# Causal attention: diagonal key blocks put together into steps of 512 columns, 34 steps per set instead of 40

## What is computed

```python
# layer 0
scores = sips_alpha[0] * jnp.tanh(raw / sips_beta[0])      # raw = q k^T
scores = scores + lam * hamming[:, None, :, :]             # feature products
scores = scores + lat
scores = jnp.where(causal[None, None], scores, -jnp.inf)
attn = jax.nn.softmax(scores, axis=-1)
# layer 1
scores = jnp.einsum('bqhd,bkhd->bhqk', q, k) * scale
scores = jnp.where(causal, -jnp.inf, scores)
attn = jax.nn.softmax(scores, axis=-1)
```

## Time and profile before

| | |
|---|---|
| median of 3 runs | 4454.76 us (4454.74 to 4455.85) |
| the profiled execution | 4471.63 us, its span 4469.8 us |
| mean granted PE clock | 0.959 of full speed |
| PE busy | 3854.6 us, 86% of the span |
| ACT busy | 3432.6 us, 77% |
| DVE busy | 2840.0 us, 64% |
| layer 0 attention | from 316 us (first tanh) to 2494 us |
| layer 1 attention | from 3032 us (first exp) to 4152 us |

### The profile page before, as it was taken

One profiled execution on the slowest core, in us unless ns is written; L12 is line 12 of the kernel. 1 busy time (PEld: TensorE's weight loads), 2 busy tenths in 40 slices (PEclk: granted clock), 3 DMA queues, 4 the chain that ended last, 5 costly groups with the idle time before them and its releaser, 6 DMA issues. The chain is left out here.

```text
span 4469.8 us, 66988 instructions
## 1 busy us (share of the span) xinstructions
PE 3854.6 (86%) x21966; PEld 1406.6 (31%) x21966; DVE 2840.0 (64%) x5324; ACT 3432.6 (77%) x3144; POOL 450.8 (10%) x407
## 2 busy tenths in 40 slices
PE   6958888888888888888888776758999999999787
PEld 2422222222222222222222463432222222222465
DVE  5637777777777777777777796872233332332588
ACT  2429999999999999999999412337999999999333
POOL 3520000000000000000000124650000000000133
PEclk9979999999999999999999888988999999999899
DMA  5851111112111112111111345562222222222332
GB/s 174 260 175 53 48 52 39 42 48 57 43 52 42 42 49 56 44 50 41 39 56 30 115 141 155 169 187 77 72 73 60 79 66 71 75 58 65 98 92 85
DMA packets 307816, 360.48 MB, mean 81 GB/s; under 512 B 56590, under 2 KB 237934, under 8 KB 307249
## 3 DMA queue, kind: packets, MB, share of 16 engines
q1 hardware_dynamic: 307508, 356.62, 27.4%
HBM read 228.15 MB, written 128.25 MB: 80 GB/s over the span
## 5 line engine op out<-in xcount | busy, mean ns | idle before, releaser
L835 DVE SCALAR_TENSOR_TENSOR att_prob<-att_tanh,alpha,ps 128x512 f32<-128x512 f32 (+3 forms) x2560 | 1569.5, 661 | 525.4 <-ACT att_tanh L775 333.9
L716 PE MATMUL ps<-att_q,att_k 99*128 99x512 bf16 (+7 forms) x5120 | 1196.7, 355 | 173.6 <-DMA att_v<-v_ones 79.1
L743 PE MATMUL ps<-att_prob,att_v 128*32 128x512 f32 (+3 forms) x10240 | 1215.1, 547 | 10.2 <-ACT att_prob L785 5.3
L775 ACT ACTIVATE att_tanh<-ps,rbeta 128x2048 f32<-128x2048 f32 (+3 forms) x640 | 1102.9, 1723 | 123.3 <-PE ps L716 123.3
L781 ACT ACTIVATE att_prob<-ps 128x1024 f32<-128x1024 f32 (+3 forms) x1280 | 1051.9, 920 | 78.4 <-PE ps L716 70.1
L785 ACT ACTIVATE att_prob<-att_prob 128x2048 f32<-128x2048 f32 (+3 forms) x640 | 1065.6, 1665 | 52.1 <-DVE att_prob L835 49.6
L725 PE MATMUL ps<-att_f,att_g 75*128 75x512 bf16 (+3 forms) x2560 | 854.0, 361 | 177.9 <-DVE att_prob L835 153.3
L716 PEld LDWEIGHTS ps<-att_q,att_k 96*128 96x128 bf16 (+1 forms) x5120 | 396.8, 99 | 1045.4 <-ACT att_prob L781 430.4
L823 DVE TENSOR_TENSOR att_prob<-att_prob,keep 128x256 f32<-128x256 f32 x512 | 211.5, 423 | 647.3 <-ACT att_prob L781 642.2
L725 PEld LDWEIGHTS ps<-att_f,att_g 75*128 75x128 bf16 x2560 | 235.7, 97 | 1060.8 <-DVE att_prob L835 1029.1
L743 PEld LDWEIGHTS ps<-att_prob,att_v 128*32 128x32 f32 x10240 | 202.5, 108 | 391.8 <-issue 147.2
(11 more groups left out here) (132 smaller groups left out, 2470.9 us busy)
## 6 DMA issues: line engine op xcount, KB each, us to landing
att_k<-k_parts SPq DMA_DIRECT2D x768, 64.0 KB
att_q<-q_parts SPq DMA_DIRECT2D x768, 64.0 KB
v_ones<-proj_vs SPq DMA_DIRECT2D x128, 256.0 KB, 3.1
att_v<-v_ones SPq DMA_DIRECT2D x128, 256.0 KB
post_o<-o_t SPq DMA_DIRECT2D x40, 512.0 KB, 5.1
att_f<-f_parts SPq DMA_DIRECT2D x384, 48.0 KB
o_t<-att_on SPq DMA_DIRECT2D x512, 32.0 KB, 1.9
q_parts<-proj_parts SPq DMA_DIRECT2D x32, 384.0 KB, 4.1
```

The costliest lines, as they stand in the source:

```text
L716: mm = pe.matmul(ps[:, bank, off:TG], keys, q_s[:, n % QU, h, off:TG], start=True, stop=True)
L743: mm = pe.matmul(ps[VW * h:VW * (h + 1), O0 + n % 2, off:TG], v_s[:, c % KU, kb % CB, h * VW:(h + 1) * VW], prob[:, S % R, h, off:TG], sta ...
L775: th.done(act.activation(tanh_s[:, S % 2, :, off:TG], ps[:, QK0:QK0 + HQ, off:TG], ACT.Tanh, scale=kn["rbeta"][:, 0:1]))
L835: sc.done(dve.scalar_tensor_tensor(prob[:, S % R, h, off:TG], tanh_s[:, S % 2, h, off:TG], kn["alpha"][:, 0:1], ps[:, E0 + h % 2, off:TG], ...
```

## The change

The order of the steps within a set comes from a new function, `even_steps`, and a step is now a list of pieces (group, key block, first query, first column, width) and a list of the columns at which a mask block lies. The 384-wide and the 128-wide diagonal block of a group form one step of 512 columns; the 256-wide blocks of groups g-1 and g (g odd) form one, placed behind the first key block of group g. So a set has 24 steps off the diagonal, 4 of the first diagonal block, 4 of 384 + 128 and 2 of 256 + 256: 34 steps, all of 512 columns. Counted from 0, groups 0 to 3 begin at steps 0, 2, 9 and 19 of the set (before: 0, 4, 12 and 24). Group 0 has its last step at step 3, group 1 at 8, group 2 at 20 and group 3 at 33.

ACT and DVE instructions of layer 0 take the whole width. PE has the same matmuls as before, per piece: in a step of two pieces there are 8 for scores, 8 for extra and 8 of masks, and 16 recorded ones for weigh. In layer 1 the two mask blocks of a pair of heads are one DVE instruction (128 x 512 elements). `normalise` does one part per step throughout in layer 0. All lookaheads, numbers of banks and buffers, and SP's order are as they were.

```diff
@@ -30,6 +30,7 @@
 GB = T // TG
 TT = TG // P
 KB = T // P
+CB = TG // P
 HQ = 4
 NHQ = H // HQ
 NF = 12
@@ -604,21 +605,39 @@
     return n
+def even_steps():
+    steps = []
+    for g in range(GB):
+        d = g * CB
+        for kb in range(d):
+            steps.append(([(g, kb, 0, 0, TG)], []))
+            if kb == 0 and g % 2 == 1:
+                steps.append(([(g - 1, d - 2, 2 * P, 0, 2 * P), (g, d + 2, 2 * P, 2 * P, 2 * P)], [0, 2 * P]))
+        steps.append(([(g, d, 0, 0, TG)], [0]))
+        steps.append(([(g, d + 3, 3 * P, 0, P), (g, d + 1, P, P, 3 * P)], [0, P]))
+    return steps
 def attend_phase(nc, kn, layer):
-    steps = [(g, kb) for g in range(GB) for kb in range((g + 1) * (TG // P))]
+    steps = even_steps()
     NST = len(steps)
+    ends = [[g for g in range(GB) if max(i for i, (ps_, _) in enumerate(steps) if any(p[0] == g for p in ps_)) == s] for s in range(NST)]
+    kept_at = [sum(1 for _, m in steps[:s] if m) for s in range(NST)]
     N_SET = B * NHQ
     N = N_SET * NST
     NG = N_SET * GB
-    ND = GB * (TG // P)
+    ND = sum(1 for _, m in steps if m)
     R = 4
     LAG = 2
     QU, KU = 3, 6
-    CB = TG // P
     QK0, E0, O0 = 0, 4, 6
     SR, FR = (QROWS, FROWS + 3) if layer == 0 else (QROWS + 3, 0)
     with ExitStack() as ctx:
@@ -654,10 +673,12 @@
         def at(S):
             it, s = divmod(S, NST)
-            g, kb = steps[s]
-            r = kb - g * CB
-            off = r * P if r > 0 else 0
-            return it, g, kb, off, r >= 0, kb == (g + 1) * CB - 1
+            return (it, s) + steps[s]
+        def blocks(t, masked):
+            first, step = masked[0], masked[1] - masked[0] if len(masked) > 1 else P
+            return t[..., first:first + step * len(masked)].rearrange("... (m n) -> ... m n", n=step)[..., 0:P]
         @block.sync
         def _(sp):
@@ -702,9 +723,9 @@
             pe.wait_ge(ones_in, 16)
             def scores(S, pair):
-                it, g, kb, off, diag, _ = at(S)
-                n, c = it * GB + g, it * GB + kb // CB
-                if kb == 0 and pair == 0:
+                it, _, pieces, _ = at(S)
+                if pieces[0][1] == 0 and pair == 0:
+                    n = it * GB + pieces[0][0]
                     pe.wait_ge(stacks_in[n % QU], (n // QU + 1) * (16 * N_LOAD))
                 if layer == 1:
                     pr.wait(pe, 2 * S + pair - 3)
@@ -712,35 +733,39 @@
                     th.wait(pe, S - 1)
                 for h in (2 * pair, 2 * pair + 1):
                     bank = QK0 + (h if layer == 0 else 2 * ((2 * S + pair) % 3) + h % 2)
-                    keys = k_s[:, c % KU, h, (kb % CB) * P:(kb % CB + 1) * P]
-                    mm = pe.matmul(ps[:, bank, off:TG], keys, q_s[:, n % QU, h, off:TG], start=True, stop=True)
+                    for g, kb, q0, col, w in pieces:
+                        n, c = it * GB + g, it * GB + kb // CB
+                        keys = k_s[:, c % KU, h, (kb % CB) * P:(kb % CB + 1) * P]
+                        mm = pe.matmul(ps[:, bank, col:col + w], keys, q_s[:, n % QU, h, q0:q0 + w], start=True, stop=True)
                 if layer == 1 or pair == 1:
                     qk.done(mm)
             def extra(S, h):
-                it, g, kb, off, diag, _ = at(S)
-                n, c = it * GB + g, it * GB + kb // CB
+                it, _, pieces, masked = at(S)
                 sc.wait(pe, S * HQ + h - 2)
-                mm = pe.matmul(ps[:, E0 + h % 2, off:TG], g_s[:, c % KU, (kb % CB) * P:(kb % CB + 1) * P], f_s[:, n % QU, h, off:TG], start=True, stop=not diag)
-                if diag:
-                    mm = pe.matmul(ps[:, E0 + h % 2, off:off + P], kn["identb"][:], kn["mask_kq"][:], start=False, stop=True)
+                for g, kb, q0, col, w in pieces:
+                    n, c = it * GB + g, it * GB + kb // CB
+                    mm = pe.matmul(ps[:, E0 + h % 2, col:col + w], g_s[:, c % KU, (kb % CB) * P:(kb % CB + 1) * P], f_s[:, n % QU, h, q0:q0 + w], start=True, stop=not masked)
+                    if masked:
+                        mm = pe.matmul(ps[:, E0 + h % 2, col:col + P], kn["identb"][:], kn["mask_kq"][:], start=False, stop=True)
                 ex.done(mm)
             def weigh(S):
-                it, g, kb, off, diag, last = at(S)
-                n, c = it * GB + g, it * GB + kb // CB
+                it, s, pieces, masked = at(S)
                 if layer == 0:
                     pr.wait(pe, S)
-                elif diag:
-                    kept.wait(pe, (it * ND + kb) * 2 + 1)
+                elif masked:
+                    kept.wait(pe, (it * ND + kept_at[s]) * 2 + 1)
                 else:
                     pr.wait(pe, S * 2 + 1)
-                if kb == 0:
-
-                    o_tr.wait(pe, n - 2)
-                for h in range(HQ):
-                    mm = pe.matmul(ps[VW * h:VW * (h + 1), O0 + n % 2, off:TG], v_s[:, c % KU, kb % CB, h * VW:(h + 1) * VW], prob[:, S % R, h, off:TG], start=kb == 0, stop=last)
+                for g, kb, q0, col, w in pieces:
+                    n, c = it * GB + g, it * GB + kb // CB
+                    if kb == 0:
+                        o_tr.wait(pe, n - 2)
+                    for h in range(HQ):
+                        mm = pe.matmul(ps[VW * h:VW * (h + 1), O0 + n % 2, q0:q0 + w], v_s[:, c % KU, kb % CB, h * VW:(h + 1) * VW], prob[:, S % R, h, col:col + w], start=kb == 0, stop=g in ends[s] and (g, kb) == [p[:2] for p in pieces if p[0] == g][-1])
                 pv.done(mm)
             scores(0, 0)
@@ -768,21 +793,19 @@
             for S in range(N + 1):
                 if S < N:
-                    it, g, kb, off, *_ = at(S)
                     if layer == 0:
                         qk.wait(act, S)
                         sc.wait(act, (S - 2) * HQ + HQ - 1)
-                        th.done(act.activation(tanh_s[:, S % 2, :, off:TG], ps[:, QK0:QK0 + HQ, off:TG], ACT.Tanh, scale=kn["rbeta"][:, 0:1]))
+                        th.done(act.activation(tanh_s[:, S % 2], ps[:, QK0:QK0 + HQ], ACT.Tanh, scale=kn["rbeta"][:, 0:1]))
                     else:
                         for pair in range(2):
                             qk.wait(act, S * 2 + pair)
                             bank = QK0 + 2 * ((2 * S + pair) % 3)
                             pv.wait(act, S - R)
-                            pr.done(act.activation(prob[:, S % R, 2 * pair:2 * pair + 2, off:TG], ps[:, bank:bank + 2, off:TG], ACT.Exp, scale=float(HD) ** -0.5))
+                            pr.done(act.activation(prob[:, S % R, 2 * pair:2 * pair + 2], ps[:, bank:bank + 2], ACT.Exp, scale=float(HD) ** -0.5))
                 if S > 0 and layer == 0:
-                    it, g, kb, off, *_ = at(S - 1)
                     sc.wait(act, (S - 1) * HQ + HQ - 1)
-                    pr.done(act.activation(prob[:, (S - 1) % R, :, off:TG], prob[:, (S - 1) % R, :, off:TG], ACT.Exp))
+                    pr.done(act.activation(prob[:, (S - 1) % R], prob[:, (S - 1) % R], ACT.Exp))
         @block.vector
         def _(dve):
@@ -793,9 +816,7 @@
             def normalise(due, count):
-                for S, part in due[:count]:
-                    it, g, *_ = at(S)
-                    G = it * GB + g
+                for S, G, part in due[:count]:
                     v = G % 2
                     if part == 0:
                         pv.wait(dve, S)
@@ -816,33 +837,33 @@
             def diagonal(S):
-                it, g, kb, off, *_ = at(S)
+                masked = at(S)[3]
                 for pair in range(2):
                     pr.wait(dve, S * 2 + pair)
-                    block = prob[:, S % R, 2 * pair:2 * pair + 2, off:off + P]
-                    kept.done(dve.tensor_tensor(block, block, kn["keep"][:].unsqueeze(1).to_broadcast([P, 2, P]), ALU.min))
+                    block = blocks(prob[:, S % R, 2 * pair:2 * pair + 2], masked)
+                    kept.done(dve.tensor_tensor(block, block, kn["keep"][:].unsqueeze(1).unsqueeze(1).to_broadcast([P, 2, len(masked), P]), ALU.min))
             def sums(S, due):
-                it, g, kb, off, *_ = at(S)
                 pv.wait(dve, S - R)
                 for h in range(HQ):
                     if h == 2:
-                        normalise(due, 2 if g <= 1 else 1)
+                        normalise(due, 1)
                     th.wait(dve, S)
                     ex.wait(dve, S * HQ + h)
-                    sc.done(dve.scalar_tensor_tensor(prob[:, S % R, h, off:TG], tanh_s[:, S % 2, h, off:TG], kn["alpha"][:, 0:1],
-                                                     ps[:, E0 + h % 2, off:TG], ALU.mult, ALU.add))
+                    sc.done(dve.scalar_tensor_tensor(prob[:, S % R, h], tanh_s[:, S % 2, h], kn["alpha"][:, 0:1],
+                                                     ps[:, E0 + h % 2], ALU.mult, ALU.add))
             due = []
             for S in range(N + LAG + 1):
-                if S > LAG and at(S - LAG - 1)[-1]:
```

(6 more changed lines are left out.)

## The result

| | before | after |
|---|---|---|
| median, us | 4455.31 (4454.74 to 4460.44) | 4270.79 (4269.56 to 4274.13) |
| span of the profiled execution | 4469.8 | 4267.4 |
| layer 0, first tanh to last exp | 2177.3 | 2010.7 |
| layer 1, first to last exp | 1119.3 | 1082.8 |
| between the layers / behind them | 538.2 / 318.5 | 537.7 / 320.1 |

The ratio is 0.9582, with a 95% interval of [0.9569, 0.9595]. The whole difference lies in the two attentions. The medians differ by 184.5 us, the profiled spans by 202.4: the profiled execution of before was longer than its timed ones, and the first experiment returns to that.

What follows compares the result with a forecast made beforehand. The prediction took ACT (3.65 us a step) to bound layer 0 and PE (1.965) layer 1, with narrow steps waiting. 177 - 5 - 15 plus 43 - 2 - 6 gave 192 us, a 4262 us median, range 4232 to 4320.

Steps and rivals of the forecast that it cites:

- Layer 0 at the full pace, 177: Layer 0: all 34 steps at ACT's 3.65 us, fixed parts and waiting gone, end at 2316.5: 177 us gained.
- Pair steps, 5: Layer 0's 96 two-piece steps: second masks and weight loads charged 0.05 us each, 5 us lost.
- normalise, nothing: DVE's normalise in layer 0, one part per step: longest 0.71 against 0.64 us slack, charged nothing; uncovered, 13 us.
- The load, 15 and 6: Group 2's load comes late for its earlier start at set boundaries: 15 us lost in layer 0, 6 in layer 1.
- Layer 1, 43: Layer 1: at PE's 1.965 us a step, a set takes 66.8 instead of 69.62 us: 43 us gained.
- The sum: Both attentions: 157 us net in layer 0 plus 35 in layer 1, 192 us in all.
- From the profile to the median: Whole kernel: 192 us taken from both the profiled 4471.6 and the median 4454.8, giving about 4280 and 4262.
- No load hindrance: Rival, group 2's load: it costs nothing, all of 220 us arrives, 4235 us; chance 0.15.
- Upper bounds with dips: Rival, set boundaries: load costs 35 + 18 us, or clock still dips behind PE's stall; together 4312 us; chance 0.14.
- Waiting kept: Rival, layer 0 pair steps: each of 96 keeps the narrow steps' 0.92 us wait, 4345 us; chance 0.08.
- Only fixed parts: Rival, both layers: only instructions' fixed parts go, 28 us in layer 0 and 24 in layer 1, 4403 us; chance 0.04.
- Slower by the half clock: Rival, both layers: half clock settles in pair steps or behind the load's stall, 279 us lost, 4542 us; chance 0.03.

Runs made afterwards that it cites:

- the first experiment: The kernel before, unchanged, profiled once more: 4458.31 us in one execution, layer 0 2162.6 us.
- the run with the later exp: The kernel before with layer 0's exp (and weigh) one step later, three tanh and five prob buffers: 4433.19 us, ratio 0.9945.
- Spread: The kernel before, 40 steps at old widths, but narrow steps of groups 1 to 3 each behind a wide one: 4566.96 us, ratio 1.0228.
- A set of 36 steps: The changed kernel with only 384 + 128 joined, each 256-wide block a step of its own: 4341.64 us, ratio 0.9725.
- the split activations: The changed kernel with ACT working on the two pieces of each pair step in two instructions: 4290.99 us, ratio 0.9624.
- the spread order: Here the kernel with narrow steps spread between wide ones, plus layer 0's exp one step later: 4478.4 us, one execution.

## Why the prediction was right, and where not

**What bounds the kernel.** Right. Behind the start of its first set layer 0 holds ACT's 3.65 us in every step not named below, layer 1 PE's 1.97.

**Layer 0 at the full pace, 177.** Right in its end: 34 x 3.65 = 124.1, and undisturbed sets took 124.3. The phase ended at 2326.7 where 2316.5 was forecast; the load and `normalise`, below, make 10.1 of that. I explained the loss as a chain PE, DVE, ACT that narrow instructions no longer cover. The runs make it two definite waits. The exp stands behind a tanh that is narrower than DVE's work (i), and the scores share their banks with the tanh, which sets 3.09 us behind a wide one (ii). The chain was right for (i) as it stands in before, and (ii) was not in it. One group's end in before, DVE and ACT:

```profile
1754.45 1.86 DVE L835 SCALAR_TENSOR_TENSOR att_prob<-att_tanh,alpha,ps 128x256 f32<-128x256 f32 x4 [0.79 <-PE ps L727]
1755.14 0.74 ACT L775 ACTIVATE att_tanh<-ps,rbeta 128x512 f32<-128x512 f32 x1
1756.35 1.06 ACT L785 ACTIVATE att_prob<-att_prob 128x1024 f32<-128x1024 f32 x1 [0.46 <-DVE att_prob L835]
1757.74 1.97 ACT L775 ACTIVATE att_tanh<-ps,rbeta 128x2048 f32<-128x2048 f32 x1 [0.34 <-PE ps L716]
...
1760.84 1.97 ACT L775 ACTIVATE att_tanh<-ps,rbeta 128x2048 f32<-128x2048 f32 x1 [0.61 <-PE ps L716]
```

Here DVE itself waited for the mask matmul, and the exp of the 256-wide step for DVE (i); both tanhs waited for scores (ii). In an undisturbed set of before ACT stands 3.05 us in 7 waits (i) and 3.43 in 8 waits (ii). Each wait also costs, as an estimate, the 0.11 us by which ACT's rows otherwise overlap (the tanh of 1.97 us at 1427.33 in the run with the later exp is followed 1.86 behind its start): 6.5 + 15 x 0.11 = 8.1, the whole of what the fixed parts leave.

At 512 everywhere the exp is due at 5.50 us against 4.86, and the next tanh at 3.65 against 3.09, so both are covered. Taking away (i) alone gave 0.8 us a set of the 8.1, because (ii) took over.

**Pair steps, 5.** Mis-sized: 0. The second mask costs no time of the step, the steps behind them are 3.65, and in layer 1 the steps are 1.97 apart with pieces too:

```profile
3401.25 1.04 PE L739 MATMUL ps<-att_q,att_k 99*128 99x512 bf16 x4
3403.22 1.04 PE L739 MATMUL ps<-att_q,att_k 99*128 99x512 bf16 x4
...
3407.15 1.04 PE L739 MATMUL ps<-att_q,att_k 99*128 99x128 bf16 x6
...
3411.09 1.04 PE L739 MATMUL ps<-att_q,att_k 99*128 99x128 bf16 x6
```

(The last two rows hold six matmuls and print the form of the first.) The Trainium skill (TensorE: Matmul & The Clock Gate, Back-to-back issue gap) gives about 81 ns for each matmul of 128 columns with its weight load, some 30 us here by the prediction's estimate. The trace does not agree: four scores of 128 and four of 384 columns took 1.05 us (row 1701.72), as four of 512, so the 0.057 taken from the earlier trace rows holds.

**normalise, nothing.** Too low: its transposes lengthen step 2 to 3.72 and two others to about 3.69. Summed over a set that is 0.21 us, 3.4 in layer 0. The 0.71 against 0.64 us of slack was the right comparison, and I should have kept its 0.07.

**The load, 15 and 6.** The mechanism and the place were right, before the first scores of group 2, on `att_v`. The sizes were 6.7 and 5.7, so that of layer 0 was more than twice too high. I had PE 1.6 to 2.9 us late in layer 0; it was 0.37 to 1.9 late at 15 boundaries, about 0.9 in the median. The start of the load was right to 0.1 us, but the issue took 17.5 to 18.3 us at 14 boundaries and 18.9 at one, where I used the one row with 18.40, and the scores followed 2.7 to 3.5 us behind instead of up to 4.17.

**Layer 1, 43.** Right. 43 - 5.7 = 37.3, and it was 36.5. Of its 2.7 us a set, 1.5 are by the prediction's estimate the fixed PE time of six steps (0.25 each), which leaves 1.2 for waiting around narrow steps. No run separates the two. Spread, the 40 steps took 68.8 instead of 69.6, so at least 0.8 hangs on the order of the narrow steps. A set of 36 steps took 68.1 to 69.4, and layer 1 1105.2 where I had 1085. Why one 256 step for each group costs that much is open.

**The sum.** With the measured terms it is 177 - 6.7 - 3.4 = 167 and 37, 204 us, against 202.4 between the two profiled spans. I had 192. So in the profile I was 10 us too low: load and pair steps were put 16 us too high (12.4 against 28), `normalise` and layer 1 some 4 too low.

**From the profile to the median.** This is the step that was wrong. The 177 us end at 2493.8 of the profiled execution and so contain its half-clock stretches. I wrote that it stood 16.9 us over the median, and still took 192 from both. The second execution of before shows that some 15 us of them are missing in a usual run. To the median belongs 204 - 17 = 187 (184.5 measured). The two errors, 10 us too little in the profile and 17 too much in the median, have opposite signs. That 4262 was only 9 us too low is in part luck; with the 17 subtracted from my 192 it would have been 4280, 9 too high.

**The rivals.** No load hindrance: refuted, 12.4 us were there. Upper bounds with dips: refuted; no half-clock stretch follows the load's stall in the windows of the sets. Waiting kept: refuted, 3.65 in pair steps. Only fixed parts: refuted by the split activations, 24 us (16 x 1.5) of 166.6 instead of nearly all; I had put them at 28, with 0.29 a step for 0.25. Slower by the half clock: the windows of all 15 sets behind the first show 1.00, so it didn't arise. Spreading the narrow steps did bring both more waits and more half clock (0.953 over the whole span). Which share of its half clock belongs to the waits stays open: with the later exp the order of before lost its half clock, the spread order kept it.

## What to carry to other kernels

This is drawn from one kernel. In a software pipeline whose engines hand over once a step, a narrow step is covered only if its neighbours' instructions last as long as the latency they stand in for. Joining narrow steps up to one common width removed every such wait at once here, where curing one wait by itself mostly uncovered the next. Before a gain read from one profiled execution is taken from a median, subtract what that execution had over the median, if the gain contains the disturbed stretches. And where a change brings a group's start forward by three steps, look at the buffers of its load: one more set of them was worth another 14.7 us (4270.79 to 4256.09).

## What the runs showed of the hardware that I had not expected

- An added ACT instruction over the same columns cost 0.15 us for the tanh and 0.09 for the exp in the split activations (2.00 - 1.85 and 1.89 - 1.80), and 0.14 where every tanh was halved (3.79 - 3.65).
- A narrow piece costs PE nothing beyond its columns: eight scores of 256 columns, or of 128 and 384, took 1.05 us, four of 512 took 1.04.
- Two executions of one program differed by 14.7 us in one phase, with a granted clock of 0.97 and 0.99 there. Their undisturbed sets took 133.9 us in both, and layer 1 1119.3 and 1120.0.
